# A graph network's Chebyshev layer: the first two terms' products of the slot rows made beside the third gather, and no scatter of the mixed rows

## The reference, cut to what matters

```python
def _cheb(x, prop, w, b):              # K = 2, 3 and 4 terms
    out = x @ w[0]; Tx0 = x; Tx1 = prop(x); out = out + Tx1 @ w[1]
    for k in range(2, K):
        Tx2 = 2.0 * prop(Tx1) - Tx0
        out = out + Tx2 @ w[k]; Tx0, Tx1 = Tx1, Tx2
    return out + b
def prop(h): return segment_sum(wn[:, None] * h[row], col, num_segments=n)
feats = [_cheb(x, prop, w2, b2), _cheb(x, prop, w3, b3), _cheb(x, prop, w4, b4)]
scale_w = softmax(concatenate(feats) @ attn_w + attn_b)
h = concatenate([feats[i] * scale_w[:, i:i + 1] for i in range(3)]) @ fus_w + fus_b
h = relu((h - mean(h)) * rsqrt(var(h) + eps) * gamma + beta)   # over all nodes
# then x3 = layernorm(x2 + h), and the GINE layer: relu(x3[src] + e) summed by dst, two linear maps, twice
```

## Time and profile before

| | us |
|---|---|
| median of 3 runs | 15155.44 |
| lowest, highest | 15152.29, 15157.25 |
| span of the profiled execution | 15156.7 |
| first and second pass with half of the dense rows each | 609.2, 610.3 |
| third pass | 510.7 |
| stage of the slots | 873.7 |
| normalization | 932.4 |

### The profile page before, as it was taken

How to read it: one execution, slowest core, us unless ns; L and a number is a source line. 1 busy time by engine, 2 the same in 40 slices (tenths; PEclk the granted TensorE clock), 3 DMA queues, 4 the chain that set the end, 5 groups by cost and what they waited for, 6 DMA issues and landing times. The chain is left out here.

```text
span 15156.7 us, 99573 instructions
## 1 busy us (share of the span) xinstructions
PE 4571.5 (30%) x22709; PEld 3654.3 (24%) x22709; DVE 8857.6 (58%) x14029; ACT 3678.8 (24%) x9401; POOL 8719.5 (58%) x8770
## 2 busy tenths in 40 slices
PE   0000012000000002000034444767049700589776
PEld 0000011000000002000033334545038600466544
DVE  8860445444444445322776778767444599658765
ACT  0000011000000001000632431656113233554431
POOL 0667777777777777777057510777654422540767
PEclk9955555555555555555555555778579855799555
DMA  6200234433343334211754333444234455677753
GB/s 209 108 4 1 65 102 129 118 111 110 112 118 110 111 115 132 86 54 50 247 177 141 119 106 112 135 124 137 82 104 134 135 190 193 223 251 244 222 165 109
DMA packets 953792, 1967.49 MB, mean 130 GB/s; under 512 B 322912, under 2 KB 330957, under 8 KB 949616
## 3 DMA queue, kind: packets, MB, share of 16 engines
q1 hardware_dynamic: 674928, 1585.65, 30.7%
q0 software_dynamic: 278272, 375.46, 10.5%
HBM read 1192.75 MB, written 783.59 MB: 130 GB/s over the span
## 5 line engine op out<-in xcount | busy, mean ns | idle before, releaser
L724 POOL DMA_INDIRECT hop_odd_raw<-hop_table,i_hop x1176 | 1112.5, 946 | 394.2 <-issue 378.5
L724 POOL DMA_INDIRECT hop_even_raw<-hop_table,i_hop x1176 | 1112.4, 946 | 387.8 <-issue 351.9
L520 POOL DMA_INDIRECT cheb_raw<-x,i_near x392 | 447.7, 1142 | 654.1 <-POOLq L89 534.9
L520 POOL DMA_INDIRECT gine_raw<-conv,i_near x392 | 396.6, 1012 | 610.5 <-POOLq L89 491.2
L1730 POOL DMA_INDIRECT own_raw<-x,i_dst x392 | 386.8, 987 | 603.0 <-POOLq L89 483.8
L981 POOL DMA_INDIRECT mid<-cheb_slots_ends_rows,dst_end x392 | 384.0, 980 | 488.2 <-DVEq L1488 371.2
L1563 PE MATMUL cheb_slots_ends_product<-folded,b_slots_ends_turned_rows 97*128 97x292 f32 (+3 forms) x3136 | 658.1, 352 | 0.0
L1563 PE MATMUL cheb_base_product<-folded,cheb_base_turned_rows 97*128 97x292 f32 x1568 | 564.4, 516 | 184.4 <-ACT cheb_base_mixed L1517 184.4
L1651 POOL TENSOR_TENSOR cheb_norm_x_mid<-cheb_norm_x_mid,coefficients 128x768 f32<-128x768 f32 x98 | 190.7, 1947 | 721.4 <-DMA cheb_norm_x_mid<-mid 721.4
L748 DVE TENSOR_TENSOR hop_odd_rows<-hop_odd_raw,hop_odd_factors 128x672 f32<-128x672 f32 x168 | 144.9, 863 | 750.5 <-DMA hop_odd_raw<-hop_table,i_hop 750.5
L748 DVE TENSOR_TENSOR hop_even_rows<-hop_even_raw,hop_even_factors 128x672 f32<-128x672 f32 x168 | 144.9, 863 | 750.0 <-DMA hop_even_raw<-hop_table,i_hop 750.0
(11 more groups left out here) (553 smaller groups left out, 22140.6 us busy)
## 6 DMA issues: line engine op xcount, KB each, us to landing
hop_odd_res<-hop_table SPq DMA_DIRECT2D x168, 336.0 KB
hop_table<-hop_odd_sums SPq DMA_DIRECT2D x168, 336.0 KB
hop_even_res<-hop_table SPq DMA_DIRECT2D x168, 336.0 KB
hop_table<-hop_even_sums SPq DMA_DIRECT2D x168, 336.0 KB
start_x_x<-x_and_map SPq DMA_DIRECT2D x98, 400.0 KB, 3.6
x<-start_x_rows SPq DMA_DIRECT2D x98, 400.0 KB
cheb_base_term<-x SPq DMA_DIRECT2D x98, 400.0 KB
mid<-cheb_base_rows SPq DMA_DIRECT2D x98, 400.0 KB, 4.4
```

The costliest lines, as they stand in the source:

```text
L520: pool.indirect_dma_start(out=raw_rows[:, b % RAW, g, :], out_offset=None, in_=table, in_offset=bass.IndirectOffsetOnAxis(ap=index[:, t:t ...
L724: pool.indirect_dma_start(out=raw_rows[:, b % RAW, g, :], out_offset=None, in_=table, in_offset=bass.IndirectOffsetOnAxis(ap=index[:, t:t ...
```

## The change

In the third pass the propagation gets the form of the first two, and a job beside it: for the slot rows the terms of power 0 and 1 are turned (VectorE copies them), multiplied, and their 292 columns stored in a new table `part`. The stage of the slots then has the terms 2 and 3 as sources and `part` as an input. The products go into banks of 4 x 256 columns, ScalarE copies both terms' turned rows, and VectorE adds the products to the loaded part. The mixed slot rows aren't scattered into `mid`. So that the next layer finds the rows of nodes with edges, the slot rows of x3 lie behind the dense ones in one table, and its gather uses the indices `i_near`, which point to a slot row where the node has one, as the second GINE pass does already.

```diff
     def __init__(self, nc, k, tag, dense, batches, sources, out, part_in=None, part_out=False, gram=None, turns=1,
-                 scatter=None, copies=("act",)):
+                 side=None, copies=("act",)):
...
-            self.product = [ph.psum(f"{self.tag}_product{n}", [P, 4, P]) for n in range(2)]
+            self.product = [ph.psum(f"{self.tag}_product{n}", [P, 4, 2 * P]) for n in range(2)]
...
-            mask = self.mask[:, i % 2, :] if self.dense else self.scatter[0].is_end[:, at]
+            mask = self.mask[:, i % 2, :] if self.dense else self.side.is_end[:, at]
...
-        x3 = table("x3", NP, C)
+        x3_all = table("x3", NP + EP, C)
+        x3, x3_slots = x3_all[0:NP, :], x3_all[NP:NP + EP, :]
+        part = table("part", EP, MIX)
...
-        hop_pass(nc, k, "cheb3", by_dst, StoreHop(nc, k, cheb_c), cheb_b, k.i_cheb, k.w_cheb, k.f_cheb, k.f_cheb[:, 0:1])
-        sources = [(0, x2_slots), (1, cheb_a), (2, cheb_b), (3, cheb_c)]
-        slot_rows(nc, k, "cheb_slots", ChebRows(nc, k, "ends", False, slots, sources, mid_slots, gram=(total, False), turns=2,
-                                                scatter=(by_dst, mid, k.N - 1), copies=("act", "dve", "act", "dve")))
+        propagate("cheb3", cheb_c, cheb_b, k.i_cheb,
+                  (ChebRows(nc, k, "put", False, slots, [(0, x2_slots), (1, cheb_a)], part, part_out=True,
+                            copies=("dve", "dve")),))
+        slot_rows(nc, k, "cheb_slots", ChebRows(nc, k, "ends", False, slots, [(2, cheb_b), (3, cheb_c)], mid_slots,
+                                                part_in=part, gram=(total, False), turns=2, side=by_dst,
+                                                copies=("act", "act")))
...
-        x3_slots, sums1, sums2 = hop_first, hop_b, cheb_a
+        sums1, sums2 = hop_b, cheb_a
...
-        edge_pass(nc, k, "gine1", by_dst, Store(nc, k, sums1), x3, by_dst.other, added=feats,
+        edge_pass(nc, k, "gine1", by_dst, Store(nc, k, sums1), x3_all, k.i_near, added=feats,
```

More of the change, by code:

```diff
@@ L1344, in __init__ @@
     def __init__(self, nc, k, tag, dense, batches, sources, out, part_in=None, part_out=False, gram=None, turns=1,
-                 scatter=None, copies=("act",)):
+                 side=None, copies=("act",)):
         self.sources = [(f"term{power}", table, power) for power, table in sources]
         self.part_in, self.part_out, self.gram, self.turns, self.copies = part_in, part_out, gram, turns, copies
+        self.side = side
         self.low = min(self.from_column(power) for _, _, power in self.sources)
@@ L1357, in __init__ @@
             self.DEPTH = 3
-        super().__init__(nc, k, tag, dense, batches, inputs, out, scatter)
+        super().__init__(nc, k, tag, dense, batches, inputs, out)
     @staticmethod
```

## The result

The changed kernel takes 15219.95 us (median of 4 runs, 15211.59 to 15226.37), the kernel before 15155.26 (of 4 too): a ratio of 1.0042, with a 95% interval of 1.0028 to 1.0056. It is slower by 65 us, where the prediction had 25 us and its range for the likeliest case ended at 15235. The profiled execution took 15211.59 us.

The account below looks back on a forecast made before the run. Pass three was taken as bound by engines waiting for each other (437 us more), the slots' stage by load landing and VectorE (412 less): +25 us, forecast 15180 us, range 15040 to 15285.

Parts of the forecast that it names:

- the likeliest case: Whole kernel: both stages go as summed, 15180 us, with its own range 15125 to 15235; chance 0.45.
- The ring: Pass three: ScalarE, VectorE and TensorE wait for each other in turn, 15.22 us a round at full clock.
- the fall of the clock: Pass three: after idling about 5.5 us TensorE runs 5.0 us at half speed, making a round 17.7 us.
- the ring doesn't form: Rival, pass three: it lasts only as long as the second pass, 610 us; kernel 14843 us; chance 0.08.
- full clock: Rival, pass three: TensorE never slows after its waits, 135 us less, kernel 15045 us; chance 0.12.
- half clock all through: Rival, pass three: TensorE stays at half speed throughout, stage 1213 us, kernel 15445 us; chance 0.06.
- The price of the half clock: Pass three: TensorE's slow work after each wait costs 2.5 us in each of 54 rounds, 135 us.
- The formula, landing and 9.9 us over two mixings: Slots' stage: period is (L + 9.9)/2 with load landing L of 7.3 us, so 8.6 us per mixing.
- The prediction's own sign of error: Wrong if pass three stays near 610 us, or if the slots' mixings lie over 10 us apart.
- the rival of late loads: Slots' stage: stored products land after 11 us, period 10.5 us, 91 us more, kernel 15271 us; chance 0.15.
- The addition out of PSUM: Slots' stage: each of VectorE's two new additions of 784 elements takes 0.97 us.
- The tail: Slots' stage: 14 us from the last mixing to the next stage, for the store's landing and the barrier.

Follow-up runs that it names:

- the own signal: Changed kernel, but in the slots' stage the stored products' load has a separate signal that only VectorE's addition waits for: 15109.86 us.
- the second bank: Changed kernel with two banks instead of one for the turned rows in pass three: 15015.67 us.

## Why the prediction was right, and where it was not

**Pass three: right.** The ring, its links and the fall of the clock came as worked out. Without the half clock a round is 15.04 us (15.22 summed), with it 17.1 to 17.8 (17.7), and with one half step 12.26 (12.84). These few tenths a round make up some 22 of the 29 us by which 948 was too long. The rivals "the ring doesn't form" and "full clock" fell by the trace, "half clock all through" too: the clock was back before the second half step, as in the earlier trace rows. The price of the half clock, 135 us in the prediction, is 111 us by the run with 9 unread products. The page of the Trainium skill that was cited (TensorE: Matmul & The Clock Gate, Loop structure matters more than you think) calls a loop with a long wait between its matmuls, there for a DMA, the bad one. The trace agrees, with a copy as what is waited for: the clock is 0.50 behind the wait of 5.18 us. Nine products that nobody reads in that wait brought it from 0.78 to 0.97 over the pass.

**The slots: the period was mis-sized.** The formula, landing and 9.9 us over two mixings, was the right loop, as the own signal shows: what it takes out of the loop is gone from the time. But the landing was 9.0 us and not 7.3. That fits a load that shares 8 us at 298 GB/s with the store issued right behind it, which I had counted only in the upper bound; no run moved the store to show it. And what follows the landing was 11.6 us and not 9.9: behind a wait of 3.09 us TensorE's products ran at half clock, 3.09 instead of 1.81 us for twelve. I had made that price a term in pass three and forgot it here. (9.0 + 11.6)/2 = 10.3, and 10.25 is the period measured over the stage; 48 × (10.25 − 8.6) = 79 us more. What part of it is the clock's alone was not tried by itself. The prediction's own sign of error, mixings over 10 us apart, was met: the rival of late loads, 0.15, came close in this stage with its period of 10.5 us, but not by its landing of 11; what its landing lacked, the slow half step added. The addition out of PSUM was 0.97 us, as taken.

**The tail: too long.** Without the scatter 4.4 us lie behind the last mixing, not 14, and the first mixing came at 31.6 us, not 35: 13 us less.

So the total, 40 us above the forecast, is −29 and −13 against +79, and some 3 us of the rest. That it lay in the likeliest case's range owes something to errors of opposite sign, and is luck in that part: a stage of 528 us where 462 were summed would by itself have put the kernel at 15246, outside that range. The rest (normalization 3 us more, next gather 1 us less) was costed at nothing.

**The rate of the transfers.** The Trainium skill (DMA: Bandwidth & Descriptors, Where 436 GB/s comes from) has about 358 GB/s for a core's HBM transfers. Over 340 us of the slots' stage the runs stay below, 301 GB/s at a DMA share of 0.91; single stretches are above, 366 GB/s over 5 us in the window shown of pass three, 403 in the earlier trace rows. It decided nothing here.

## What to carry to other kernels

When work is moved into a stage with idle engines, look at where it is put in each engine's program, not only at the engines' idle time: here one engine's copies behind its chain cost 376 us more than ahead of it. TensorE's waits of 3 and 5 us had two prices here, the wait and the slow products behind it; whoever counts the second in one stage has to count it in each. Let every consumer wait for the transfer that it reads, not for the batch of loads that comes with it.

## What the hardware showed unexpectedly

After waits of 2.43 and 2.42 us in two successive rounds with the second bank, the granted clock stayed at 1.00 once (from 11008.46) and fell to 0.50 within half a microsecond the other time (from 11020.71). Before the first wait TensorE had worked for 16.3 us, with no wait for the copies between, before the second for 9.8 us; whether that is the reason was not tried. The windows behind the two waits:

```profile
11009.00:11018.29 9.29, 9.29 (x45) 6.91 (x43) 2.81 (x7) 6.01 (x21) 4.26 (x6) 1.00 0.76 255
...
11021.00:11022.00 1.00, 1.00 (x5) 0.84 (x4) 0.33 (x1) 0.00 (x0) 0.69 (x2) 0.50 0.25 57
```

And eighteen unread product instructions of 4.59 us in a wait, with 0.76 us of idle time left, held the clock at 1.00 for stretches of 250 us.
